# Routed attention block: the bias term of the scores summed on VectorE and brought in by two passes with ones

## The chip, the cores and the metric

The kernel runs on one core of a Trainium2 chip. The metric is the device time of one execution in microseconds (us); the median of three runs of the kernel before is 603.29 us (601.7 to 603.42).

## The reference

Four sequences of 2048 tokens of width 256 pass an attention layer and then a soft mixture of experts, each with a residual and a layer norm. All is fp32. What matters here:

```python
def _mlp(x, W1, b1, W2, b2):
    h = jax.nn.gelu(x @ W1 + b1, approximate=False)
    return h @ W2 + b2
q, k, v = (_mlp(x, ...) for each of q, k, v)
scale = np.sqrt(N_EMBD * BLOCK_SIZE).astype(np.float32)
scores = jnp.einsum('bid,bjd->bij', q, k) / scale
scores = scores * jnp.tril(jnp.ones((T, T)))          # no softmax
out = jnp.einsum('bij,bjd->bid', scores, v)
x = _layernorm(x + (layernorm of out) * ln_w + ln_b)
...
xn = _layernorm(x, ln_gamma, ln_beta)
logits = jnp.einsum('bnd,des->bnes', l2norm(xn) * scale, l2norm(mu))
dispatch = softmax(logits, over the tokens); combine = softmax(logits, over the 256 slots)
slot_in = jnp.einsum('bnd,bnes->besd', xn, dispatch)
slot_out = gelu(slot_in @ w1 + b1) @ w2 + b2
x = _layernorm(x + jnp.einsum('besd,bnes->bnd', slot_out, combine))
```

As the scores have no softmax, attention is linear: out of a token is q times the running sum of k^T v over the earlier tokens (the state), plus a part within its own chunk. The bias of q's second layer makes a term that is the same for every query: gamma_j = b2q . k_j, so each output row also gets the sum of gamma_j v_j over all earlier tokens j. That sum is what the change deals with.

## The kernel before

Tokens are cut into 64 tiles (chunks) of 128 tokens, 16 to a sequence. Four chunks make a group (512 tokens, `GT = 4`), four groups a sequence (`GB = 4`), 16 groups in all. The kernel is two blocks with a barrier of all engines between them: attention, then routing with the experts and the output. Each engine has its own program, written out by hand; order between engines comes from semaphores alone, and an engine that waits holds up all behind it.

In attention, `body(g, ...)` runs on each engine once for each group: it projects group g (hidden layers for k, q, v, then k and v themselves) and attends group a = g - 1 between these. TensorE's order is: hidden k, scores of a, hidden q, `chunk` 0, hidden v's first half, `chunk` 1, second half, k of chunks 0 and 1, `chunk` 2, k of chunks 2 and 3, `chunk` 3, v. Products are split three ways (`split3`: hi x hi, hi x lo, lo x hi, in fp32r). `chunk` adds the product with the state (`read_state`, from `state_hi` and `state_lo`, which ScalarE rounds and VectorE splits off after each `update_state`), the product of the masked scores with v (`attend_chunk`), then updates the state.

The gamma term: column D of `k_tok` is gamma. ScalarE rounds it (`gam_hi`, L607), VectorE takes the rest (`split_gamma`, L1057). `carry` (L848) runs three passes of gamma, spread over 128 columns as weights, with the 256 columns of v, into the output tile of the next chunk; ScalarE has copied the sum so far from the tile before it (`preload`, L612), so that each tile starts with the sum over all earlier chunks. VectorE then takes the statistics of the output tile pair (`pair_statistics`), weights it (`weight_out`) and adds it to x (`add_out`). GpSimd makes the low halves of the hidden v (`split_hv`), of x (`split_x`), of k (`split_ktok`) and of v (`split_v`), adds ln_b, and takes the powers for 1/sqrt (`invert_o`, and `invert_z` with `invert_x1` for the norm of z = x + attention). Twelve of the bodies stand in a hardware loop; the first two and the last two do not.

At the end of attention, `last_chunks` (TensorE) and `last_body` (VectorE) handle the last group, with the first routing steps among them: `scale_tokens(k, q)` on VectorE multiplies group k by 1/std and the routing norm's weight (L213), `add_beta` on GpSimd adds its bias (L220), `norms` on ScalarE, `floor_norms` on VectorE and `invert_norms` on GpSimd give the l2 norm, `turn_xn`, `round_xnT` and `split_xnT` turn the tokens. The last act of GpSimd in the block is `add_beta(1, 1)`, which waits for VectorE's `scale_tokens(1, 1)`. In the routing block, `route(0, first=True)` still carries what is left of groups 14 and 15: VectorE's `finish_out(15, ...)`, `shift_z` for group 14 after turning tile 3 (L1611), and ScalarE's `apply_z` of group 14 at tiles 4 to 7 (L1432), between its exponentials.

## Time and profile before

| | us |
|---|---|
| median of three runs | 603.29 |
| the profiled execution, its own time | 603.0 |
| its span | 601.3 |
| attention block | 0 to 404.3 of the span |
| routing block, experts and output | 404.3 to 601.3 |

The profiled execution is 0.3 us under the median, and 1.7 us of its time lie outside its span. The page gives the busy share of each engine and a strip of 40 slices (15 us each) with the busy tenths and TensorE's granted clock. A view by line gives the cost of one instruction; the timeline gives start, length and, in brackets, the idle time ahead of it with what ended it. Matmul lengths overlap (an entry of 0.28 us starts 0.12 us after the one ahead of it), so the cost of a pass is read from the distance of starts.

### The profile page before, as it was taken

How to read it: one execution, taken by the hardware profiler on the slowest of the kernel's cores; microseconds unless marked ns; L12 is line 12 of the kernel's file. 1: busy time of each engine (PE TensorE's matmuls, PEld its weight loads, DVE VectorE, ACT ScalarE, POOL GpSimd, SP SyncE). 2: the span in 40 equal slices, each digit the busy share in tenths (PEclk: the TensorE clock that was granted, in tenths of full speed). 3: DMA queues.
4: the chain of work that ended last, by engine and by line, in shares of the span. 5: the costliest groups of instructions: out<-in, count | busy, mean ns of one | idle time of the engine just before them, and what ended most of it. 6: DMA issues, size and time to landing. Idle time of an engine off the chain costs nothing. (4 is left out here: it accounts for less than half of the span.)

```text
span 601.3 us, 11764 instructions
## 1 busy us (share of the span) xinstructions
PE 579.7 (96%) x3844; PEld 531.7 (88%) x3844; DVE 478.5 (80%) x1012; ACT 392.8 (65%) x888; POOL 344.2 (57%) x359
## 2 busy tenths in 40 slices
PE   7989999999999999999999999977999999999995
PEld 5879999989999998999998999967899999988884
DVE  5698789788797897887978979878887777447786
ACT  3755766666767667667676766555877777535774
POOL 1738568577595585675956856466644444104443
PEclk9999999999999999999999999999899999999999
DMA  7324134042141340422413403204455555832444
GB/s 229 79 71 105 19 89 87 21 106 38 68 105 17 87 89 22 99 37 68 105 17 87 104 8 65 35 5 82 67 75 76 74 76 73 137 47 74 166 147 174
DMA packets 163473, 47.04 MB, mean 78 GB/s; under 512 B 139470, under 2 KB 159340, under 8 KB 163436
## 3 DMA queue, kind: packets, MB, share of 16 engines
q1 hardware_dynamic: 163424, 46.57, 35.4%
q8 instruction: 20, 0.33, 0.2%
q14 instruction: 17, 0.14, 0.1%
q10 hardware_dynamic: 12, 0.00, 0.0%
HBM read 21.39 MB, written 8.39 MB: 50 GB/s over the span
## 5 line engine op out<-in xcount | busy, mean ns | idle before, releaser
L511 POOL TENSOR_TENSOR h_lo<-xn_all,h_hi 128x512 fp32r<-128x512 f32 x32 | 41.4, 1292 | 114.2 <-ACT xn_all L595 114.1
L593 ACT ACTIVATE h_hi<-bank,bias_col 128x512 fp32r<-128x512 f32 x96 | 66.3, 691 | 32.9 <-PE bank L713 29.1
L711 PE MATMUL bank<-xnT_hi,w_hi 128*128 128x512 f32 x188 | 76.1, 405 | 0.0
L712 PE MATMUL bank<-xnT_lo,w_hi 128*128 128x512 f32 x188 | 74.4, 396 | 0.0
L713 PE MATMUL bank<-xnT_hi,w_lo 128*128 128x512 f32 x188 | 74.1, 394 | 0.0
L1510 PE MATMUL bank<-xn_all,e_tok 128*128 128x257 f32 x256 | 65.8, 383 | 0.0
L1084 DVE TENSOR_TENSOR state_lo<-bank,state_hi 128x512 fp32r<-128x512 f32 x57 | 39.2, 688 | 32.2 <-ACT state_hi L630 32.2
L630 ACT CAST state_hi<-bank 128x512 fp32r<-128x512 f32 x57 | 33.5, 588 | 37.1 <-PE bank L843 37.1
L1600 DVE STREAM_TRANSPOSE e_turn<-e_tok 128x256 f32<-128x256 f32 x64 | 40.5, 638 | 20.8 <-ACT e_tok L1414 20.2
L1588 PE MATMUL bank<-w_sb,ET_all 128*128 128x256 f32 x256 | 55.4, 379 | 0.0
L1414 ACT ACTIVATE e_tok<-bank,shift,xinv 128x256 f32<-128x256 f32 x64 | 36.2, 566 | 29.0 <-PE bank L1500 26.1
L1588 PEld LDWEIGHTS bank<-w_sb,ET_all 128*128 128x128 f32 x256 | 48.6, 190 | 6.6
L1498 PE MATMUL bank<-mu_hi,xnT_hi 128*128 128x256 f32 x128 | 47.5, 371 | 5.9 <-ACT e_tok L1414 3.1
L1510 PEld LDWEIGHTS bank<-xn_all,e_tok 128*128 128x128 f32 x256 | 44.5, 191 | 3.9
L237 POOL TENSOR_TENSOR xinv<-n_low,minus_half 128x4 f32<-128x4 f32 x16 | 18.2, 1140 | 51.0 <-DVE n_low L232 51.0
L517 POOL TENSOR_TENSOR ktok_lo<-xn_all,ktok_hi 128x512 fp32r<-128x512 f32 x32 | 38.2, 1194 | 11.4 <-ACT ktok_hi L610 11.4
L713 PEld LDWEIGHTS bank<-xnT_hi,w_lo 128*128 128x128 f32 x188 | 35.4, 188 | 8.7
L621 ACT CAST v_hi<-xn_all 128x512 fp32r<-128x512 f32 x32 | 19.9, 621 | 32.9 <-DVE xn_all L1064 32.9
L523 POOL TENSOR_TENSOR v_lo<-xn_all,v_hi 128x512 fp32r<-128x512 f32 x32 | 40.5, 1288 | 1.3 <-ACT v_hi L621 1.3
L506 POOL TENSOR_TENSOR x_all<-x_all,lnb_rows 128x512 f32 (+1 forms) x32 | 40.8, 1303 | 0.0
L711 PEld LDWEIGHTS bank<-xnT_hi,w_hi 128*128 128x128 f32 x188 | 35.4, 188 | 5.9
L712 PEld LDWEIGHTS bank<-xnT_lo,w_hi 128*128 128x128 f32 x188 | 35.4, 188 | 5.6
(188 smaller groups left out, 2054.3 us busy)
## 6 DMA issues: line engine op xcount, KB each, us to landing
x_all<-in_L_attn_x SPq DMA_DIRECT2D x16, 512.0 KB, 3.7
kT<-k_turn SPq DMA_DIRECT2D x128, 64.0 KB, 2.5
ET_all<-e_turn SPq DMA_DIRECT2D x64, 128.0 KB, 3.8
xn_all<-in_xT SPq DMA_DIRECT2D x15, 512.0 KB, 4.4
out<-xn_all SPq DMA_DIRECT2D x15, 512.0 KB, 3.0
w_sb<-in_L_ffn_w SPq DMA_DIRECT2D x2, 512.0 KB, 6.0
xn_all<-in_L_ffn_w SPq DMA_DIRECT2D x2, 512.0 KB, 6.8
xn_all<-in_xT SPq DMA_DIRECT2D x2, 256.0 KB, 3.8
```

The costliest lines, as they stand in the source:

```text
L506: pool.tensor_tensor(xp, xp, lnb_rows[:, :].unsqueeze(1).to_broadcast([P, 2, D]), ALU.add).then_inc(xb_ready, 1)
L511: pool.tensor_tensor(h_lo[:, V_SLOT, m, :], hv[:, m, :], h_hi[:, V_SLOT, m, :].bitcast(F32), ALU.subtract).then_inc(hv_split, 1)
L523: pool.tensor_tensor(v_lo[:, pair, :], v_tok[:, pair, :], v_hi[:, pair, :].bitcast(F32), ALU.subtract).then_inc(v_split, 1)
L593: nc.scalar.activation(h_hi[:, h_slot(j, n), m, :], ps, ACT.Gelu, bias=bias(n, m))
L711: nc.tensor.matmul(ps, w[0], xs[0], start=start, stop=False, skip_group_check=shared)
L712: nc.tensor.matmul(ps, w[0], xs[1], start=False, stop=False, skip_group_check=shared)
L713: return nc.tensor.matmul(ps, w[1], xs[0], start=False, stop=stop, skip_group_check=shared)
L1084: nc.vector.tensor_tensor(lo[:, :, :], state_halves, hi[:, :, :].bitcast(F32), ALU.subtract).then_inc(state_split, 1)
L1498: nc.tensor.matmul(ps, hi, mu_hi[:, kb, :], start=(kb == 0), stop=False)
L1510: last = nc.tensor.matmul(fold_ps(b)[s][:, 0:D + 1], e_tok[:, t % 4, s * P:(s + 1) * P], xn[q][:, t % GT, :], start=(t == 0), stop=(t == T ...
L1588: last = nc.tensor.matmul(mix_ps[k % 2][t][:, 0:D], ET_all[:, k, GT * s + t, :], so[:, k // GB, s, :], start=(s == 0), stop=(s == SB - 1))
L1600: nc.vector.transpose(e_turn[q % 2][:, :, :, t % GT, :], e_tok[:, t % 4, :].rearrange("p (s r f) -> p f s r", s=SB, f=FOUR)).then_inc(e_tu ...
```

## The change

- `carry` is now two passes. VectorE keeps `v_sum`: for each of the 128 token places the sum of gamma times v over all earlier chunks (`sum_v` and `close_sum`, one instruction of 128x256 for each chunk). ScalarE rounds it in pairs (`round_vsum`), GpSimd takes the low half (`split_vsum`), and TensorE multiplies both by a matrix of ones into the chunk's own output tile. `preload`, `gam_hi` and `split_gamma` are gone.
- `chunk` puts the carry between its other passes; for the first chunk of a sequence it updates the state first and attends second. TensorE now waits itself (`z_ready`) until the output tiles are free.
- GpSimd's body starts with `split_vsum(a, 0)`, and only then comes the power chain of z (`invert_z`, `invert_x1`), which was at the end of the body before.
- At the end of attention: tokens of group 1 are scaled on GpSimd in two instructions (`divide_tokens`, `weight_tokens`) in place of VectorE's four; `add_beta(1, 1)` moves behind the barrier, and GpSimd's `add_ln_b` for the last group one body ahead.
- In routing, VectorE's `shift_z` of group 14 comes after tile 2 (ahead of `scale_tokens(3, 3)`) and not after tile 3, and `split_xnT(1, 1)` stands ahead of `weight_out`.
- At the start, `mark_out` (two fp32 products of 512 columns) is `warm_up` (three), and the causal mask is 128 wide and not 512.

```diff
@@ gpsimd
+                def split_vsum(g, m):
+                    pool.wait_ge(vsum_rounded, 2 * g + m + 1)
+                    pair = slice(2 * m, 2 * m + 2)
+                    pool.tensor_tensor(vsum_lo[:, pair, :], v_sum[:, pair, :], vsum_hi[:, pair, :].bitcast(F32),
+                                       ALU.subtract).then_inc(vsum_split, 1)
+                def divide_tokens(k, q):
+                    pool.wait_ge(x1_ready, GT * k + 3 * GT)
+                    pool.wait_ge(r2_ready, k + 3)
+                    pool.wait_ge(hv_split, 2 * GROUPS)
+                    pool.tensor_tensor(xn[q][:, :, 0:D], x1_all[:, GT * k:GT * k + GT, :],
+                                       r2_all[:, GT * k:GT * k + GT].unsqueeze(2).to_broadcast([P, GT, D]),
+                                       ALU.mult).then_inc(tok_divided, 1)
+                def weight_tokens(q):
+                    pool.wait_ge(tok_divided, 1)
+                    pool.tensor_tensor(xn[q][:, :, 0:D], xn[q][:, :, 0:D],
+                                       g_rows[:, :].unsqueeze(1).to_broadcast([P, GT, D]), ALU.mult
+                                       ).then_inc(tok_scaled, GT)
                 def body(g, j, ba, attend=True, project=True, settle=True, more=True):
                     a = g - 1
                     if not project:
+                        split_vsum(a, 1)
+                        weight_tokens(1)
+                        return
+                    if attend:
+                        split_vsum(a, 0)
+                    if attend and settle:
+                        invert_z(pool, a - 1, j % 2)
+                        invert_x1(pool, a - 1, j % 2)
+                    split_hv(g, 0)
+                    if attend:
+                        invert_o(pool, a, 0)
+                    if not more:
+                        add_beta(pool, 0, 0)
+                    if attend:
+                        split_vsum(a, 1)
+                    split_hv(g, 1)
...
+                    if not more:
+                        divide_tokens(1, 1)
+                    split_ktok(g, 0)
...
-                    if attend and project and more:
-                        invert_z(pool, a, (j - 1) % 2)
-                        invert_x1(pool, a, (j - 1) % 2)
@@ scalar
-                    nc.scalar.copy(gam_hi[:, :], k_tok[:, :, D]).then_inc(gam_rounded, 1)
-                def preload(ba, i):
...
+                def round_vsum(g, m):
+                    act.wait_ge(v_summed, GT * g + 2 * m + 1)
+                    pair = slice(2 * m, 2 * m + 2)
+                    nc.scalar.copy(vsum_hi[:, pair, :], v_sum[:, pair, :]).then_inc(vsum_rounded, 1)
                     hidden(g, j, WK1, 0)
+                    if attend:
+                        round_vsum(a, 0)
                     hidden(g, j, WK1, 1)
...
                         follow(0)
+                    if attend:
+                        round_vsum(a, 1)
@@ tensor
-                def carry(a, ba, i):
...
+                def carry(a, c, start):
+                    pe.wait_ge(vsum_split, 2 * a + c // 2 + 1)
+                    if isinstance(a, int) and a == 0 and c == 1:
+                        pe.wait_ge(ones_rounded, 1)
+                    nc.tensor.matmul(out_tile(c), ones_r[:, :], vsum_hi[:, c, :], start=start, stop=False,
+                                     skip_group_check=True)
+                    nc.tensor.matmul(out_tile(c), ones_r[:, :], vsum_lo[:, c, :], start=False, stop=False,
+                                     skip_group_check=True)
                 def chunk(a, ja, ba, c, p):
                     i = GT * ja + c
-                    if 0 < i < TB - 1:
-                        pe.wait_ge(preloaded, PB * ba + i)
                     if i == 0:
-                        pe.wait_ge(z_ready, GT * a + 2)
+                        update_state(a, c, True)
+                    if c % 2 == 0:
+                        pe.wait_ge(z_ready, GT * a + c + 2)
+                    if i == 0:
                         last = attend_chunk(a, c, True, True)
                     elif c == 0:
-                        read_state(ba, i, c, p, False)
+                        read_state(ba, i, c, p, True, False)
+                        carry(a, c, False)
                         last = attend_chunk(a, c, False, True)
                     else:
-                        attend_chunk(a, c, False, False)
-                        last = read_state(ba, i, c, p, True)
+                        attend_chunk(a, c, True, False)
+                        carry(a, c, False)
+                        last = read_state(ba, i, c, p, False, True)
@@ vector
-                def split_gamma(g):
...
+                def sum_v(g, j, c):
+                    dve.wait_ge(v_biased, 2 * g + c // 2 + 1)
+                    if not (isinstance(g, int) and g == 0):
+                        dve.wait_ge(v_summed, GT * g + c)
+                        dve.wait_ge(vsum_split, 2 * g)
...
+                        last = nc.vector.scalar_tensor_tensor(out=v_sum[:, c + 1, :], in0=v_tok[:, c, :], scalar=gamma,
+                                                              in1=v_sum[:, c, :], op0=ALU.mult, op1=ALU.add)
...
+                    if attend:
+                        sum_v(a, ja, 1)
+                        sum_v(a, ja, 2)
                     split_h(g, j, WQ1, 0)
...
                         follow(0)
+                        close_sum(a, ja)
                     split_h(g, j, WQ1, 1)
...
-                    split_gamma(g)
+                    sum_v(g, j, 0)
@@ routing
+                add_beta(pool, 1, 1)
                 invert_o(pool, GROUPS - 1, 0)
...
-                        if first and t == 3:
+                        if first and t == 2:
                             shift_z(dve, a - 1, 1 - p)
```

## Rows read from the trace of the kernel before

**Rows 1.** The page's second part: TensorE's busy tenths in 40 slices of the span

```profile
PE   7989999999999999999999999977999999999995
```

**Rows 2.** Stretches: busy us (count) of PE, PEld, DVE, ACT, POOL; clock; DMA

```profile
280.00:300.00 20.00, 20.00 (x146) 18.77 (x146) 17.64 (x39) 13.47 (x27) 15.66 (x17) 1.00 0.33 79
```

**Rows 3.** Timeline of TensorE: one carry of three passes, and what follows it

```profile
206.37 0.28 PE L711 MATMUL bank<-v_hi,gam_hi 128*128 128x256 f32 x1
...
206.71 0.40 PE L711 MATMUL bank<-xnT_hi,w_hi 128*128 128x512 f32 x1
```

**Rows 4.** Groups by line, 0 to 400 us: busy, mean ns of one | idle before

```profile
L713 PE MATMUL bank<-v_hi,gam_lo 128*128 128x256 f32 x60 | 16.6, 277 | 0.0
...
L213 DVE SCALAR_TENSOR_TENSOR xn_all<-x_all,r_all,g_rows 128x256 f32<-128x256 f32 x4 | 1.7, 476 | 0.0
```

**Rows 5.** VectorE's gam_lo: duration ns min/median/max

```profile
L1057 DVE TENSOR_TENSOR gam_lo<-xn_all,gam_hi x16: 340/354/1297, 26.6 to 391.1; 128x4 fp32r<-128x4 f32 x16
```

**Rows 6.** Timeline of VectorE, from gam_lo to the state of the next chunk

```profile
222.48 1.28 DVE L1057 TENSOR_TENSOR gam_lo<-xn_all,gam_hi 128x4 fp32r<-128x4 f32 x1
...
227.35 0.69 DVE L1079 TENSOR_TENSOR masked_lo<-bank,masked_hi 128x512 fp32r<-128x512 f32 x1
...
230.26 0.69 DVE L1084 TENSOR_TENSOR state_lo<-bank,state_hi 128x512 fp32r<-128x512 f32 x1 [1.06 <-ACT state_hi L630]
```

**Rows 7.** Timeline of GpSimd, the same stretch

```profile
222.45 2.51 POOL L523 TENSOR_TENSOR v_lo<-xn_all,v_hi 128x512 fp32r<-128x512 f32 x2
...
227.16 1.01 POOL L205 TENSOR_TENSOR r_all<-ve_x,minus_half 128x4 f32 x1 [0.18 <-POOL ve_x L203]
232.73 1.28 POOL L511 TENSOR_TENSOR h_lo<-xn_all,h_hi 128x512 fp32r<-128x512 f32 x1 [4.57 <-ACT xn_all L595]
...
236.26 1.30 POOL L511 TENSOR_TENSOR h_lo<-xn_all,h_hi 128x512 fp32r<-128x512 f32 x1 [1.45 <-ACT xn_all L595]
```

**Rows 8.** Timeline of TensorE: chunk 1 reads the state

```profile
231.54 0.28 PE L711 MATMUL bank<-state_hi,h_hi 128*128 128x256 f32 x1
```

**Rows 9.** Timeline of TensorE: first chunk of a sequence, with the wait ahead of it

```profile
132.22 0.38 PE L711 MATMUL bank<-v_hi,masked_hi 128*128 128x256 f32 x1 [0.19 <-DVE masked_lo L1079]
```

**Rows 10.** Timeline of GpSimd at the end of attention and over the barrier

```profile
401.86 2.17 POOL L220 TENSOR_TENSOR xn_all<-xn_all,b_rows 128x1024 f32<-128x1024 f32 x1 [3.51 <-DVE xn_all L213]
404.34 0.20 POOL L1355 MEMSET blank<- 128x1 f32 x4 [0.31 <-POOLq L261]
```

**Rows 11.** Timeline of TensorE: last pass of attention, first of routing, two waits in it

```profile
401.78 0.28 PE L713 MATMUL bank<-v_hi,masked_lo 128*128 128x256 f32 x1
404.58 0.36 PE L1498 MATMUL bank<-mu_hi,xnT_hi 128*128 128x256 f32 x1 [2.53 <-POOL blank L1355]
...
420.51 0.39 PE L1498 MATMUL bank<-mu_hi,xnT_hi 128*128 128x256 f32 x1 [3.06 <-ACT e_tok L1414]
...
422.97 0.58 PE L1498 MATMUL bank<-mu_hi,xnT_hi 128*128 128x256 f32 x1 [0.35 <-DVE xnT_lo L257]
```

**Rows 12.** Stretches of 4 us at the start of routing, columns as in rows 2

```profile
404.00:408.00 4.00, 3.42 (x17) 3.45 (x18) 3.55 (x9) 2.00 (x8) 1.49 (x11) 0.61 0.64 142
...
420.00:424.00 4.00, 3.14 (x15) 2.42 (x16) 3.91 (x9) 4.00 (x13) 0.41 (x1) 0.74 0.76 110
424.00:428.00 4.00, 4.00 (x24) 3.68 (x24) 2.94 (x8) 3.35 (x12) 2.62 (x6) 0.83 0.15 19
```

**Rows 13.** Timelines of VectorE, GpSimd and ScalarE where z of group 14 is shifted

```profile
417.47 1.80 DVE L181 SCALAR_TENSOR_TENSOR nm_z<-st_z,r_z 128x4 f32<-128x4 f32 x1
...
417.09 2.17 POOL L220 TENSOR_TENSOR xn_all<-xn_all,b_rows 128x1024 f32<-128x1024 f32 x1
...
419.31 0.60 ACT L189 ACTIVATE x_all<-x_all,nm_z,r_z 128x256 f32<-128x256 f32 x1 [5.27 <-DVE nm_z L181]
```

**Rows 14.** Timeline of TensorE at the start

```profile
2.98 3.78 PE L776 MATMUL bank<-causal,ident 128*128 128x512 f32 x4 [2.98 <-POOL causal L491]
...
7.25 1.96 PE L724 MATMUL bank<-xnT_hi,w_hi 128*128 128x512 f32 x4 [0.28 <-ACT bias_col L647]
```

166 lines of the change are left out of this document (82 added, 84 removed).

## The prediction, made before the changed kernel was run

> **What bounds the kernel now.** I read the busy strip first: TensorE is at nine tenths or more in nearly every slice from the third to the twenty-fifth, dips to seven once, around 400 us, and is full again after [rows 1]. The stretches say how full: in attention TensorE is busy 20.00 of 20 us at the whole clock, while VectorE has some 17.6, ScalarE 13.5, GpSimd 15.7 [rows 2]. So inside attention a pass that TensorE no longer runs is time won, as long as no other engine comes too late; and what the others get or lose matters only through their lateness. Then I read the timeline for the exceptions. In the first chunk of a later sequence TensorE waits 0.19 us for the masked scores [rows 9]. At the barrier between the blocks it stands from 402.06 (401.78 + 0.28) to 404.58; soon after, for 3.06 us ahead of 420.51, and for 0.35 us ahead of 422.97 [rows 11]. The clock, whole (2.4 GHz) in attention, is granted at 0.61 over the 4 us after the first long wait and at 0.74 and 0.83 over those after the second: part of each is spent at the lower level of 1.2 GHz [rows 12].
>
> **The change part by part.**
>
> *The passes.* A carry of three passes starts at 206.37 and the next work at 206.71: 0.34 us [rows 3], or 0.115 us a pass. 60 carries run before, as each of the three passes stands 60 times [rows 4]. After, again 60 (15 of 16 chunks, four sequences), of two passes: two passes of the same 256 columns. The starts of neighbours are 0.115 to 0.12 us apart, so 0.235 us. 60 x (0.343 - 0.235) = **-6.5 us** (ends: -6.3 and -6.9).
>
> *VectorE.* gone: `gam_lo`, 16 times, 0.34 us at least and 1.30 at most [rows 5]. New: one instruction for each chunk, nearest row `scale_tokens`, 128x256 of two SBUF tensors, 0.476 us, 0.41 from start to start in a row of four [rows 4]. Of four in a group one stands in gam_lo's place; three fill idle time: ahead of the split of hidden q, and after the state's split, where VectorE idles 1.06 us [rows 6].
> What of it is late? gam_lo needs 0.08 us of work but took 1.28: it started at 222.48, 0.03 us after GpSimd's v_lo (two of 1.26 us from 222.45), and ended as the first of these ended [rows 6, 7]. An instruction of VectorE that reads two tensors of SBUF stands until GpSimd's running one is over. The new sums are of that kind. The one in gam_lo's place inherits that wait and adds 0.4 us of work, so the masked scores, at the end of the same unbroken run of VectorE, come 0.4 us later: 228.44 and not 228.04 [rows 6]. TensorE wants them after reading the state, near 228.7: it fits by 0.25 us. Two more sums follow (0.85 us), the split of hidden q (0.6), then the state: without waits VectorE is there at 229.9, ScalarE hands over the rounded state at about 230.7 (230.26 + 0.4), so the state is split at 231.35. TensorE reads it at 231.54 [rows 8], 0.11 us earlier after the change (0.345 of passes go ahead of it, 0.235 come): 231.43. GpSimd's power chain runs 1.7 us later than now (the new split of 1.29 ahead of it and 0.4), so its last power of 1.01 us [rows 7] can fall on the second sum and cost up to 1 us, of which about 0.8 is free. I take 0.04 us in each of 14 groups, **+0.5** (ends 0 and +4).
>
> *First chunks.* The state update now goes ahead of the masked product, so the 0.19 us [rows 9] go, three times, -0.5. But there is no reading of the state ahead of chunk 0 there, so the state of chunk 1 is wanted 0.6 us sooner than in other groups, and the same 0.4 us make it late by 0.2 to 0.5: +0.6. Together **+0.1**. In the very first attended group VectorE also has the routing matrix to split; the two sums delay the state by about 0.25 us: **+0.25**.
>
> *ScalarE and GpSimd.* ScalarE loses 56 copies and 16 small ones and gets 32 of about 0.6 us in idle time; the first of each group stands ahead of the second half of hidden k, which is wanted only after the masking. GpSimd gets 32 splits of 1.29 us (like v_lo), 2.6 us a group: one ahead of the power chain, where 4.57 us of idle time follow, one ahead of the second `split_hv`, where it idles 1.45 [rows 7]. Behind the first wait (for ScalarE) stand only z's powers, wanted on VectorE 4 us later. I take nothing; without that cover they would cost 2.6 us a group.
>
> *The start.* `warm_up` is three fp32 products for two: 3.78 us for two [rows 14], so 1.9 more, begun 0.6 us sooner as the mask is smaller. First hidden starts at about 8.3 and not 7.25 [rows 14], but its four passes then may run at the whole clock (1.96 us now, half that). **+0.3** (ends -0.3 and +1).
>
> *The last group.* GpSimd's list is fuller: `divide_tokens` (2.2 us, like `add_beta`, [rows 10]), ln_b and the splits of the sums. `round_vsum` of group 15 stands on ScalarE ahead of the first turned tokens and the state, and waits for its sum: the state of the second chunk comes 1.1 us later. TensorE, whose chain there already runs from state to state, ends that much later, less the passes saved and what it waits for now: **+0.8** (ends 0 and +2).
>
> *The barrier.* Now GpSimd's add_beta (401.86 to 404.03) is last, and routing starts 0.31 us later, TensorE 0.24 after that [rows 10, 11]. After, add_beta is behind the barrier, the token scaling ends near 402.3, and TensorE itself is last. Its gap of 2.52 us becomes 0.31 + 0.24, some 0.6: **-1.9** (ends -2.2 and -1).
>
> *Opening of routing.* VectorE is the bound from 410 to 423. `shift_z` took 1.80 us for four columns, because GpSimd's add_beta ran from 417.09 to 419.26, and ScalarE stood 5.27 us for it [rows 13]. One tile earlier it meets only short steps of the powers: -1.5 on VectorE. ScalarE is free 3.6 us sooner, but then TensorE waits for VectorE's split of group 2's tokens, so 3.06 + 0.35 of waiting shrink by 1.5 and not by 3.4. Against that, add_beta(1) now starts with VectorE's `scale_tokens(2, 2)` and can hold it 2.2 us, of which 0.7 lands in VectorE's run (the rest in its idle places); TensorE waits 1.3 us for the turned tokens where now it runs slowly: **-0.8** (ends -3.1 and +1.5).
>
> The Trainium skill (SBUF, State Buffer, section on SBUF's two separate sides) says that GpSimd and a VectorE operation with two SBUF inputs share a port pair as an exclusive lock, held for a whole instruction, whoever starts first. That speaks against putting sums on VectorE and splits on GpSimd. By that rule the trace agrees (gam_lo, and `shift_z`), and the sum above already has it; its full reach is rival C.
> The skill (TensorE: Matmul & The Clock Gate, Part 1) has the clock fall to half with idleness; by that rule the trace agrees at both long waits [rows 11, 12]; shorter waits would make it rival A, and 592.1.
>
> *Sum.* -6.5 + 0.5 + 0.1 + 0.25 + 0.3 + 0.8 - 1.9 - 0.8 = -7.25. On the profiled execution's 603.0 that gives 595.75; the median of the runs is 0.3 higher: **596.0**.
>
> **The rivals.**
> A. *The clock stays whole and the opening runs through.* The lowered clock costs 4 x 0.39 = 1.6 us after the first long wait and 4 x (0.26 + 0.17) = 1.7 after the second [rows 12]. If the shorter waits leave the clock up, and VectorE isn't held by add_beta, the opening gives 3.1 and one stretch of lowered clock 1.6 more: 596.0 - 2.3 - 1.6 = 592.1. Against it: 2.5 us of waiting remain ahead of group 2.
> B. *Half of the gain is waited away.* The state's split is late by 0.3 us in each of 14 groups (+4.2): 600.2, with the tail at its upper end 601.5. For it: the margin in an ordinary group is 0.1 us. Against: 0.8 us of VectorE's idle time is there for a wait.
> C. *Slower.* Both sums after the masks wait out a GpSimd instruction each (1.29 for the new split, or a power of 1.01) and the masked scores come after their 0.25 us of margin. Two whole waits are 2.3 us, 0.8 free: 1.5 us late, 14 times 21 us less the repair by later slack, at 0.9 a group 12.6: about 608. The decision point is 0.45 us of lateness a group, where the 6.5 us are gone. Against: the power chain's short steps leave gaps, and v_lo is over by then.
> D. *It doesn't do what it says.* TensorE's time doesn't follow the passes (the ones product costs more than a pass with v, or other waits close up behind it): 603.
>
> **How the numbers follow.** Forecast (594 to 598) 0.50; A (591.5 to 594) 0.13; B (598 to 601.5) 0.22; D 0.08; C 0.07. The range 593.0 to 600.5 holds the forecast, the nearer parts of A and most of B, about 0.8. A measurement of this kernel tells 0.3% (1.8 us) from no change: faster (under 601.5) 0.85, same 0.08, slower 0.07.
>
> **What would show it.** Passes: in the steady stretches TensorE stays at 20.00 of 20 us and a group takes 0.43 us less. Masks and state: a wait of TensorE for state_lo in the list of waits, over 1 us in total, is B; over 10 us, C. Barrier: gap under 1 us. Opening: nm_z of group 14 under 0.4 us, ScalarE's wait for it gone, TensorE's longest wait there on the split of the tokens. Start: first hidden near 8.3 us. The prediction is wrong if VectorE's sums take far more than 0.5 us each, or if the ones product's starts are more than 0.12 us apart.

## The result

| | before | changed |
|---|---|---|
| median of the runs | 603.07 (5 runs) | 598.42 (5 runs) |
| lowest to highest | 601.70 to 603.42 | 596.35 to 598.54 |
| profiled execution, its own time | 603.0 | 598.5 |
| its span | 601.3 | 596.8 |

The changed kernel takes 0.9914 of the time before, 95% interval 0.9891 to 0.9938: 4.65 us less, where 7.1 were forecast. The page's strip of busy tenths of TensorE and of its granted clock, 40 slices of 15 us (before: [rows 1]):

```profile
PE   8989999999999999999999999887999999999995
...
PEclk9999999999999999999999999999899999999998
```

The same bound as before: TensorE is full through attention and dips at the border to the routing. The stretches of the changed kernel (columns: busy us and count of PE, PEld, DVE, ACT, POOL, then clock, DMA share and GB/s); the first answers to [rows 2], the last stands at the same clock times as one of [rows 12]:

```profile
280.00:300.00 20.00, 20.00 (x143) 18.73 (x142) 18.34 (x39) 13.75 (x25) 18.27 (x19) 1.00 0.35 79
...
416.00:420.00 4.00, 1.85 (x7) 1.78 (x8) 4.00 (x10) 2.02 (x8) 1.56 (x2) 0.74 0.81 112
420.00:424.00 4.00, 4.00 (x24) 3.60 (x23) 2.47 (x7) 2.98 (x10) 2.68 (x6) 0.83 0.48 66
```

TensorE still has 20.00 of 20 us, GpSimd has gone from 15.66 to 18.27, VectorE from 17.64 to 18.34. The new work by groups of lines, from 0 to 400 us (busy us, mean ns of one, idle time before it):

```profile
L882 PE MATMUL bank<-vsum_hi,ones_r 128*128 128x256 f32 x60 | 17.0, 283 | 2.1 <-POOL vsum_lo L531 2.1
L884 PE MATMUL bank<-vsum_lo,ones_r 128*128 128x256 f32 x60 | 16.9, 281 | 0.0
...
L531 POOL TENSOR_TENSOR vsum_lo<-v_sum,vsum_hi 128x512 fp32r<-128x512 f32 x32 | 41.3, 1289 | 0.6 <-ACT vsum_hi L641 0.6
...
L1107 DVE SCALAR_TENSOR_TENSOR v_sum<-xn_all,v_sum 128x256 f32<-128x256 f32 x44 | 24.3, 552 | 2.7 <-DVE v_sum L1107 1.3
```

60 carries of two passes, and GpSimd's split keeps TensorE waiting for 2.1 us in all.

**Where the 4.5 us of span come from.** I cut both spans at TensorE's starts of the scores of each group, at the first pass of the routing, and at the first pass behind the routing's last long wait. The forecast for each stretch is the prediction's own sum, its passes laid out by stretch: a carry before is 0.343 us, after 0.235, so a group whose chunks carry four times on both sides gains 0.43. In a sequence's first group four carries become three (0.67), in its last group three become four (0.09).

| stretch | before | changed | difference | forecast |
|---|---|---|---|---|
| start to the first scores | 29.04 | 29.40 | +0.36 | +0.3 |
| first attended group | 26.21 | 26.48 | +0.27 | -0.4 |
| 13 groups of the steady part | 312.55 | 308.37 | -4.18 | -4.7 |
| group with the last projections | 22.39 | 24.09 | +1.70 | -0.4 |
| last scores to TensorE's end in attention | 11.87 | 12.26 | +0.39 | +0.7 |
| that end to the first pass of the routing | 2.52 | 0.53 | -1.99 | -1.9 |
| to the pass behind the last long wait | 18.39 | 17.02 | -1.37 | -0.8 |
| the rest | 178.33 | 178.65 | +0.32 | 0 |

So one stretch misses by 2.1 us, the groups of the steady part by 0.5, the first attended group by 0.7, and the opening of the routing does better by 0.6.

One of these differences is hardly the change's. Behind the barrier the profile before has some 3 us at the half clock (1.2 GHz) [rows 12]. A run further down, the kernel before without the third pass of its carries, has the same routing code and waits 2.63 us at the barrier, and there the clock stays whole. Its first pass of the routing, its pass behind the last long wait, and its stretch behind the barrier (columns as in rows 2):

```profile
398.22 0.36 PE L1500 MATMUL bank<-mu_hi,xnT_hi 128*128 128x256 f32 x1 [2.63 <-POOL blank L1357]
...
415.34 0.58 PE L1500 MATMUL bank<-mu_hi,xnT_hi 128*128 128x256 f32 x1 [0.39 <-DVE xnT_lo L257]
...
398.00:402.00 4.00, 3.78 (x31) 3.73 (x31) 3.91 (x10) 2.79 (x10) 1.80 (x10) 1.00 0.78 167
```

That is 17.12 us where the table has 18.39 for the kernel before (the run with full weights has 17.12 too). So 1.27 of the opening's 1.37 us are the lower clock of the execution before. With the clock whole behind the barrier on both sides the opening gained 0.1.

The experiments take the stretches in turn. Each experiment is set against the changed kernel's profile or against the kernel before on the same chip.

### The profile page after: what moved, and what is told of

Read it like the earlier page. It is cut to its first block and busy times, and to the rows that moved or that the text cites. A ratio compares the mean times of both kernels' runs of the same rounds, so it can differ in the third digit from the quotient of the medians.

```text
span 596.8 us, 11673 instructions
## 1 busy us (share of the span) xinstructions
PE 575.5 (96%) x3786; PEld 527.4 (88%) x3786; DVE 490.3 (82%) x1054; ACT 390.9 (65%) x848; POOL 391.8 (66%) x393
## 5 line engine op out<-in xcount | busy, mean ns | idle before, releaser
L1471 ACT ACTIVATE e_tok<-bank,shift,xinv 128x256 f32<-128x256 f32 x64 | 36.1, 564 | 31.3 <-PE bank L1557 25.7
L525 POOL TENSOR_TENSOR v_lo<-xn_all,v_hi 128x512 fp32r<-128x512 f32 x32 | 42.7, 1354 | 1.3 <-ACT v_hi L646 1.3
L531 POOL TENSOR_TENSOR vsum_lo<-v_sum,vsum_hi 128x512 fp32r<-128x512 f32 x32 | 41.3, 1289 | 0.6 <-ACT vsum_hi L641 0.6
```

The lines of the kernel that those rows point to most:

```text
L525: pool.tensor_tensor(v_lo[:, pair, :], v_tok[:, pair, :], v_hi[:, pair, :].bitcast(F32), ALU.subtract).then_inc(v_split, 1)
L531: pool.tensor_tensor(vsum_lo[:, pair, :], v_sum[:, pair, :], vsum_hi[:, pair, :].bitcast(F32), ALU.subtract).then_inc(vsum_split, 1)
```

## The experiments

### The group with the last projections

GpSimd (POOL) and TensorE (PE) of the changed kernel, timelines:

```profile
375.87 2.20 POOL L220 TENSOR_TENSOR xn_all<-xn_all,b_rows 128x1024 f32<-128x1024 f32 x1
378.02 1.28 POOL L531 TENSOR_TENSOR vsum_lo<-v_sum,vsum_hi 128x512 fp32r<-128x512 f32 x1
...
379.35 0.39 PE L882 MATMUL bank<-vsum_hi,ones_r 128*128 128x256 f32 x1 [1.68 <-POOL vsum_lo L531]
```

In this group alone `add_beta` of group 0 (2.20 us) stands ahead of the split that TensorE's third chunk reads. In a steady group that split ends only 0.36 us ahead of the pass that reads it (changed kernel):

```profile
210.46 1.29 POOL L531 TENSOR_TENSOR vsum_lo<-v_sum,vsum_hi 128x512 fp32r<-128x512 f32 x1
...
212.11 0.28 PE L882 MATMUL bank<-vsum_hi,ones_r 128*128 128x256 f32 x1
```

The experiment only swaps the two:

```diff
-                    if not more:
-                        add_beta(pool, 0, 0)
                     if attend:
                         split_vsum(a, 1)
                     split_hv(g, 1)
+                    if not more:
+                        add_beta(pool, 0, 0)
```

> The changed kernel with one reorder: in the body of the last group GpSimd adds beta of group 0 (2.20 us) behind the split of the sums and the hidden v, not ahead of them. Theory (a wait of 1.68 us at chunk 2 of that body is lost for good, as the body took 24.09 us where 22.39 stood before): that body takes 22.4 us or less and the time falls by 1.5 to 1.9 us against the changed kernel. Rival (later work, the turned tokens of group 0 above all, wants beta so soon that the wait moves there): the time falls by under 0.5 us.

Measured: 595.95 us (4 runs; before, on the same chip, 602.41), 0.9889 of the kernel before, 0.9846 to 0.9932; span 594.0. The same timelines:

```profile
375.14 1.29 POOL L531 TENSOR_TENSOR vsum_lo<-v_sum,vsum_hi 128x512 fp32r<-128x512 f32 x1
...
377.75 2.21 POOL L220 TENSOR_TENSOR xn_all<-xn_all,b_rows 128x1024 f32<-128x1024 f32 x1
...
376.79 0.28 PE L882 MATMUL bank<-vsum_hi,ones_r 128*128 128x256 f32 x1
```

The wait is gone and the group takes 22.16 us instead of 24.09. Nothing behind it gives that back. The +1.70 is this order of two instructions.

### What the pass itself is worth

The kernel before, with the third pass of each carry (`gam_lo` times `v_hi`) left out; its carried term lacks that small part:

```diff
-                    split3(out_tile((i + 1) % GT),
-                           (gam_hi[:, c:c + 1].to_broadcast([P, P]), gam_lo[:, c:c + 1].to_broadcast([P, P])),
-                           (v_hi[:, c, :], v_lo[:, c, :]), False, False, shared=True).then_inc(carried, 1)
+                    gam = gam_hi[:, c:c + 1].to_broadcast([P, P])
+                    nc.tensor.matmul(out_tile((i + 1) % GT), gam, v_hi[:, c, :], start=False, stop=False,
+                                     skip_group_check=True)
+                    nc.tensor.matmul(out_tile((i + 1) % GT), gam, v_lo[:, c, :], start=False, stop=False,
+                                     skip_group_check=True).then_inc(carried, 1)
```

> The kernel before with the third pass of each carry (low half of gamma times v) left out, so a small part of the carried sum is missing; nothing is added to VectorE, ScalarE or GpSimd. This is what the pass alone is worth. Theory: 60 x 0.115 = 6.9 us less, all of it, because TensorE never waits in attention: 596.2. Rival (other engines close up behind TensorE): less than 4 us.

Measured: 596.92 us (8 runs, 595.05 to 599.69; before, on the same chip, 602.41), 0.9906 of the kernel before, 0.9881 to 0.9932; the profiled execution is one of the fast ones, 595.35, with a span of 593.6 against 601.3. The groups of 24.33 us take 23.87: there a pass that goes is won in full, 0.115 us each. In the first group of a later sequence the wait for the masked scores takes 0.1 of 0.46 us back. From the first to the last scores 57 passes bring 6.09 us, 0.107 each, and 60 at that are 6.4, close to the forecast's 6.5; the medians differ by 5.5. The gain of the changed kernel's steady group, 24.33 to 24.11, is half of that. Something else in the group must have become slower, and without a wait: in the list of what TensorE waited for in the changed kernel, from 29 to 376 us (us in total, times, longest), all three are in the first attended group:

```profile
PE bank L873 <- DVE x_all L1159: 1.4, 1, 1.4
PE bank L742 <- DVE state_lo L1135: 0.5, 1, 0.5
PE bank L844 <- DMA kT<-k_turn: 0.2, 1, 0.2
```

### The pace of the passes around the carry

The cause shows in the distance of starts. v's projection is 24 passes of 256 columns; its first pass and the pass behind its last, before:

```profile
241.86 0.28 PE L711 MATMUL bank<-w_hi,h_hi 128*128 128x256 f32 x1
...
244.58 0.40 PE L711 MATMUL bank<-xnT_hi,w_hi 128*128 128x512 f32 x1
```

and in the changed kernel:

```profile
239.72 0.28 PE L742 MATMUL bank<-w_hi,h_hi 128*128 128x256 f32 x1
...
242.58 0.39 PE L742 MATMUL bank<-xnT_hi,w_hi 128*128 128x512 f32 x1
```

2.72 us and 2.86, 113.3 ns and 119.2 ns a pass, the same passes at the same clock. In the kernel before, ten of the 13 steady groups have the fast pace, and the groups on either side of them. The three without a carry ahead of the projection have 117.9 there. k's projection (12 passes of 258 columns, twice a group) went from 120.0 to 122.5 ns. Added up from start to start over one group of 24.33 us, the carries fell from 1.37 to 0.95 us, v's projection rose from 2.72 to 2.86, k's two from 2.87 to 2.94, and all other passes together changed by less than 0.01: -0.43 and +0.21 are the -0.22. Five runs look for the reason: weights of one column spread over 128 ahead of the projection, or the addresses of the buffers, which moved with the new ones and the smaller mask.

The kernel before, with full weights in the carry (a block of k's tokens in gamma's place, so the carried term is another quantity):

```diff
-   (gam_hi[:, c:c + 1].to_broadcast([P, P]), gam_lo[:, c:c + 1].to_broadcast([P, P])),
+   (ktok_hi[:, c, 0:P], ktok_lo[:, c, 0:P]),
```

> The kernel before, with the carry's three passes on a full 128x128 block of k as weights and not on gamma spread from one column; the carried term is thus something else than the reference asks. Theory (spread weights ahead of v's projection make its fast pace): the carry takes 0.36 us and not 0.345, the projection of v 2.86 us and not 2.72, and a group 24.50 us and not 24.33. Rival (what makes the pace is a carry standing there, its pass into the output bank, whatever its weights): 2.72 and 24.33 stay.

Measured: 604.38 us (one run), span 602.7. v's projection has 117.9 ns everywhere, the group 24.50 us instead of 24.33. So in the kernel before, the carry's weights right ahead of it do make the fast pace.

The changed kernel, with a spread column of ones:

```diff
-                    nc.tensor.matmul(out_tile(c), ones_r[:, :], vsum_hi[:, c, :], start=start, stop=False,
+                    nc.tensor.matmul(out_tile(c), ones_r[:, 0:1].to_broadcast([P, P]), vsum_hi[:, c, :], start=start, stop=False,
```

(and the same for `vsum_lo`).

> The changed kernel, the matrix of ones read as one column spread over 128 (stride 0), as gamma was before. In the kernel before, the 24 passes of v's projection start 0.1133 us apart where a carry of spread gamma stands right ahead of them, and 0.1185 where none does; in the changed kernel 0.119 always. Theory 1 (the spread weights themselves run faster): the carry's two passes take 0.230 us and not 0.24, the projection stays at 0.119 because reading and updating the state stand between. Theory 2 (spread weights anywhere in the chunk put TensorE in a faster pace for what follows): the projection of v falls to 0.1133 and a group to 23.96 us. Rival (pace has nothing to do with weights): nothing changes, group 24.11.

Measured: 597.93 us (one run), span 596.2; the projections stay at 119.2 and 122.5 ns, a group is 24.05 instead of 24.11, by slightly closer starts of the state's reading and update (0.02 us each) and of the carries (0.01). Only in the three groups that end a sequence, with no update of the state ahead of v's projection, does that go to 118.7. Here the carry doesn't stand right ahead of v's projection, the state's reading does. So the next run puts every fourth chunk's carry there (`carry_last` is the carry's two passes with a spread column of ones):

```diff
+                    elif c == GT - 1:
+                        attend_chunk(a, c, True, False)
+                        read_state(ba, i, c, p, False, False)
+                        if i < TB - 1:
+                            update_state(a, c, False)
+                        carry_last(c).then_inc(chunk_done, 1)
+                        return
```

> The changed kernel, with the carry of every fourth chunk put back where the kernel before had its own: behind the state's update, right ahead of v's projection, and with one column of ones spread over 128 as its weights. Theory 1 (the 113 ns passes of v's projection come from spread weights right ahead of them): the projection is back at 113 ns a pass and 2.72 us in the groups that have this carry, against 2.86 us in the changed kernel; a group of kind 1 and 2 goes from 24.11 to 23.97 us, three of four groups gain 0.14 us, and the span falls by some 1.5 us (10 to 11 groups). Theory 2 (addresses of the buffers, which the change moved, set the pace of v's projection): it stays at 119 ns, and the groups stay at 24.11.

Measured: 597.65 us (one run), span 595.9. The projection goes to 118.5 ns and not to 113.3. The first theory falls in this form.

The addresses: the new buffers behind the others, and small ones of the same total size in their place, so that all buffers of hidden layers and chunks stand where they stood before the change (not all of the moved declarations are shown).

```diff
-            v_sum = asb("v_sum", [P, GT, D])
-            vsum_hi = asb("vsum_hi", [P, GT, D], F32R)
-            vsum_lo = asb("vsum_lo", [P, GT, D], F32R)
-            ones_r = asb("ones_r", [P, P], F32R)
+            warm = asb("warm", [P, GT])
+            mu_n2 = asb("mu_n2", [P, SB])
+            mu_inv = asb("mu_inv", [P, SB])
...
             causal = asb("causal", [P, P])
+            ones = asb("ones", [P, P])
+            mu_diag = asb("mu_diag", [P, SB, P])
...
             state_lo = asb("state_lo", [P, KB, D], F32R)
-            warm = asb("warm", [P, GT])
+            v_sum = asb("v_sum", [P, GT, D])
+            vsum_hi = asb("vsum_hi", [P, GT, D], F32R)
+            vsum_lo = asb("vsum_lo", [P, GT, D], F32R)
+            ones_r = asb("ones_r", [P, P], F32R)
...
```

> The changed kernel with its new buffers (the sums, their halves, the ones) declared behind the others and small ones put in their place, so that the hidden layers' buffers stand at the addresses of the kernel before. Theory 2 (addresses set the pace): k's projection, 122.5 ns a pass in the changed kernel and 120.0 before, goes back to 120.0 (-0.03 us on each of two stretches a group, -0.06 a group, -0.8 in all), and v's from 119.2 to 117.9 (-0.03 a group). Theory 1 (only the order of the passes and their weights matter): both stay at 122.5 and 119.2, and the group stays at 24.11.

Measured: 595.38 us (one run), span 593.7. First pass of a k projection and the pass behind its last, changed kernel and then this run:

```profile
210.28 0.28 PE L742 MATMUL bank<-m_hi,h_hi 128*128 128x258 f32 x1
...
211.75 0.29 PE L742 MATMUL bank<-v_hi,masked_hi 128*128 128x256 f32 x1
```

```profile
208.94 0.28 PE L742 MATMUL bank<-m_hi,h_hi 128*128 128x258 f32 x1
...
210.38 0.28 PE L742 MATMUL bank<-v_hi,masked_hi 128*128 128x256 f32 x1
```

k's projection is back at 120.0 ns, v's at 117.9, the group at 24.05 and 23.33 (24.11 and 23.39). From first to last scores that is 0.74 us (386.58 - 28.38 = 358.20, against 358.94). That part of the loss was the addresses. The rest of the 3.1 us of span is a shorter start (28.38 against 29.40, which differs from run to run: 28.2 to 29.5 in the kernels with this start) and the clock, below.

Both together, with the edits of the run on `add_beta` and of one on the routing (below):

> The changed kernel with four edits at once: the add of beta of group 0 behind the two splits; the split of transposed group 2 ahead of the statistics in the routing; the hidden layers' buffers at the addresses of the kernel before; and every fourth chunk's carry last, with a spread column of ones, right ahead of v's projection. The runs so far show that a spread carry right ahead gave 113 ns passes in the kernel before and only 118.7 in the changed one. If that was because the addresses were others (the two causes act together), the projection is now at 113.3 ns and 2.72 us in 11 groups, a group of kind 1 and 2 takes 23.92 us, and the median is some 1.2 us under that of the next run, near 592.3. If the fast passes have to do with the gamma weights or with v as what is moved through, and not with the spread alone, they stay at 117.9, the group at 24.04, and the median is that of the next run.

Measured: 593.49 us (4 runs; before 601.88), 0.9855 of the kernel before, 0.9836 to 0.9874. Last pass of the carry, first of v's projection, and the pass behind its last:

```profile
262.44 0.28 PE L882 MATMUL bank<-vsum_lo,ones_r 128*128 128x256 f32 x1
262.56 0.29 PE L742 MATMUL bank<-w_hi,h_hi 128*128 128x256 f32 x1
...
265.37 0.39 PE L742 MATMUL bank<-xnT_hi,w_hi 128*128 128x512 f32 x1
```

2.81 us: 117.1 ns, against 117.9 without a spread carry ahead at these addresses. The spread alone and the old addresses don't bring 113.3 back. What is left is what the kernel before had and no run of the changed one has: gamma's own column as the weights, v as what is moved through, or the next chunk's output tile as the target. Which of the three is open, as no run separates them, and why TensorE's starts should hang on any is open too. The size is known: 24 x 4.6 ns, 0.11 us, in ten groups of the steady part, 1.1 us.

### Is GpSimd's order in the steady group needed?

The change puts the split of the first sums ahead of z's powers. Put back:

```diff
-                    if attend:
-                        split_vsum(a, 0)
                     if attend and settle:
                         invert_z(pool, a - 1, j % 2)
                         invert_x1(pool, a - 1, j % 2)
+                    if attend:
+                        split_vsum(a, 0)
```

> The changed kernel with GpSimd's z chain (3.1 to 3.3 us in all) ahead of the split of the first sums, as the kernel before had it at a group's end. Rival C of the prediction, that TensorE gets its operands too late once GpSimd has more ahead of them: the split then starts when the chain has ended, some 3.3 us later than now; its lead over the pass that reads it (split's end 201.66, pass at 204.14: 2.5 us) turns into a wait of 0.6 to 1.0 us in each group whose first chunk carries (11 groups), none in the others, where the second chunk reads it 5.9 us after the scores' start: the span is 6 to 10 us longer, 604 to 607, which takes back all that the change gave. If the margin is larger than that (nothing is late), the span stays at 596.8.

Measured: 609.69 us (one run), span 608.0, 11.2 more than the changed kernel and 6.7 more than the kernel before. GpSimd and TensorE, and TensorE's line in the list of waits from 29 to 390 us:

```profile
207.07 1.01 POOL L205 TENSOR_TENSOR r_all<-ve_x,minus_half 128x4 f32 x1 [0.18 <-POOL ve_x L203]
208.04 1.43 POOL L531 TENSOR_TENSOR vsum_lo<-v_sum,vsum_hi 128x512 fp32r<-128x512 f32 x1
...
209.52 0.39 PE L882 MATMUL bank<-vsum_hi,ones_r 128*128 128x256 f32 x1 [0.77 <-POOL vsum_lo L531]
```

```profile
PE bank L882 <- POOL vsum_lo L531: 8.5, 11, 0.8
```

11 waits of 0.77 us, and each such group is 1.0 longer (24.11 to 25.13), so a wait costs a third more than the list says: around it the starts are further apart (the state's six passes with the wait take 1.64 us instead of 0.71, the carry 0.35 instead of 0.24). The groups without such a wait lose 0.2. With this order the change is slower than no change, which is rival C of the prediction at another place: the sums' split, not the masks, behind GpSimd's powers.

### The barrier and the opening of the routing

TensorE at the end of attention and in the opening, changed kernel, only the rows with a wait (before: [rows 11]):

```profile
392.98 0.39 PE L873 MATMUL bank<-v_hi,ktok_hi 128*128 128x256 f32 x1 [1.22 <-DVE h_lo L1135]
394.43 0.36 PE L882 MATMUL bank<-vsum_hi,ones_r 128*128 128x256 f32 x1 [0.47 <-POOL vsum_lo L531]
401.13 0.36 PE L1555 MATMUL bank<-mu_hi,xnT_hi 128*128 128x256 f32 x1 [0.53 <-POOL blank L1411]
...
403.52 0.55 PE L245 MATMUL bank<-ident,xn_all 128*128 128x128 f32 x3 [0.73 <-POOL xn_all L220]
...
418.15 0.58 PE L1555 MATMUL bank<-mu_hi,xnT_hi 128*128 128x256 f32 x1 [2.55 <-DVE xnT_lo L257]
```

*The add of beta put back ahead of the barrier:*

```diff
                         weight_tokens(1)
+                        add_beta(pool, 1, 1)
                         return
...
-                add_beta(pool, 1, 1)
                 invert_o(pool, GROUPS - 1, 0)
```

> The changed kernel with the add of beta of group 1 put back ahead of the barrier between attention and routing, on GpSimd, behind the product with gamma. Theory (prediction: the barrier's gap of 2.52 us was this add, and moving it takes 1.9 of it away): the add takes 2.2 us before the barrier, the first logits pass comes 1.9 to 2.2 us later, TensorE's gap at the barrier goes from 0.53 to some 2.5; behind it the 0.73 us wait for the transposed group's beta goes, and VectorE's scale of four tiles falls from 3.62 us to 1.7, so that the net loss is 1 to 1.5 us. Rival: the gap has another floor (the barrier itself, or the product with gamma), and the first pass moves by less than 0.5 us.

Measured: 597.21 us (one run), span 595.5. Its GpSimd, TensorE and VectorE:

```profile
399.37 2.19 POOL L220 TENSOR_TENSOR xn_all<-xn_all,b_rows 128x1024 f32<-128x1024 f32 x1
...
402.12 0.36 PE L1555 MATMUL bank<-mu_hi,xnT_hi 128*128 128x256 f32 x1 [1.67 <-POOL blank L1412]
...
401.91 1.67 DVE L213 SCALAR_TENSOR_TENSOR xn_all<-x_all,r_all,g_rows 128x256 f32<-128x256 f32 x4 [2.52 <-PEq L261]
```

From the last scores to the routing's first pass it takes 13.94 us against 12.79: the move is worth 1.15 at the barrier, not the 1.9 that the prediction gave it. The gap is 1.67 here and was 2.53 before [rows 11], though the add is the same and stands at the same place. Before, it ended 1.97 us after TensorE's last pass (404.03 against 402.06, [rows 10, 11]), here 1.11 us (401.56 against 400.45): the tokens' scaling ahead of it is two GpSimd products, the first made long before, and no longer VectorE's. That is the other 0.8 of the 1.99. Behind the barrier the changed kernel pays the add: 0.73 us of TensorE's wait, and VectorE's scaling of four tiles, which takes 1.67 us here, runs from 400.93 to 404.55 there. To the pass behind the last long wait it is 16.17 us against 17.02. Net, the move brought 0.3 us. That this run's span is 1.3 us under the changed kernel's is the clock again: no half clock falls in behind its wait of 2.55 us, where the changed kernel's profile has it (below).

*The shift of group 14 one tile later, as before:*

```diff
-                        if first and t == 2:
+                        if first and t == 3:
                             shift_z(dve, a - 1, 1 - p)
```

> The changed kernel with group 14's shift (nm_z) put back to the fourth token tile of the routing, where it was before. If the earlier place made the gain of the opening (prediction, with 0.8 us in all and 0.4 of it for the shift): the shift starts behind the scale of four tiles and meets GpSimd's add of beta, so it takes 1.8 us instead of 0.12; ScalarE waits some 3 to 5 us for it instead of 1.5, and the stretch from the first logits pass to the pass behind the last big wait, 17.02 us in the changed kernel and 18.39 before, is 18.2 to 18.5: the span is 1.2 to 1.5 us over that of the changed kernel. Rival: the gain of the opening comes from the split of the second transposed group going ahead of pair 0's output and from the beta that went before the barrier; then the stretch stays within 0.4 us of 17.02.

Measured: 599.33 us (one run), span 597.6. VectorE and ScalarE, of the changed kernel and then of this run:

```profile
412.40 0.12 DVE L181 SCALAR_TENSOR_TENSOR nm_z<-st_z,r_z 128x4 f32<-128x4 f32 x1
...
412.56 0.60 ACT L189 ACTIVATE x_all<-x_all,nm_z,r_z 128x256 f32<-128x256 f32 x1 [1.50 <-DVE nm_z L181]
```

```profile
413.31 1.80 DVE L181 SCALAR_TENSOR_TENSOR nm_z<-st_z,r_z 128x4 f32<-128x4 f32 x1
...
412.93 2.17 POOL L220 TENSOR_TENSOR xn_all<-xn_all,b_rows 128x1024 f32<-128x1024 f32 x1
...
415.15 0.60 ACT L189 ACTIVATE x_all<-x_all,nm_z,r_z 128x256 f32<-128x256 f32 x1 [5.27 <-DVE nm_z L181]
```

The same four columns, 0.12 and 1.80 us, and the long one ends with GpSimd's add (412.93 + 2.17 = 415.10). The eleventh token tile of the routing starts 24.42 us after the first instead of 22.48. The half clock lasts longer in this run, some 7 us against 3:

```profile
416.00:420.00 4.00, 3.65 (x13) 0.50 0.72 104
```

(416 to 420 us: busy us and count of PE, clock, DMA share, GB/s.) But the delay is VectorE's and not the clock's: its split for the ninth tile ends 18.81 us after the first pass, and 16.96 in the changed kernel. So the shift's place is worth 1.9 us. The moved add of beta takes 0.85 of it back. If the two simply add up, the rest of the change costs another 0.9 in the opening, as at the same clock only 0.1 is left; no run takes that apart. The Trainium skill (SBUF, State Buffer, section on SBUF's two separate sides) has GpSimd and a VectorE instruction with two SBUF inputs share a port pair as an exclusive lock for a whole instruction. By that rule the trace agrees in each of these pairs (1.80 us against 0.12 for the shift, 3.62 against 1.67 for the scaling), and it is what to look for when four columns take as long as an instruction of another engine.

*The split of group 2's tokens ahead of the statistics.* The 2.55 us ahead of 418.15 are VectorE's: it runs two statistics and a transpose first. The experiment has the edit on `add_beta` of group 0 too:

```diff
                         if first and t == 4:
+                            split_xnT(dve, 2, 2)
+                        if first and t == 4:
                             z_summed(dve, a, 0)
...
-                        if t % GT == 1 and not (last and q == GB - 1) and not (first and q == 0):
+                        if t % GT == 1 and not (last and q == GB - 1) and not (first and q <= 1):
                             split_xnT(dve, k + 1, (q + 1) % GB)
```

> The changed kernel with two edits that the traces point to. One is that of the run before on this matter (the add of beta of group 0 behind the two splits that TensorE waits for). The other: in the routing of group 0, VectorE splits the transposed tokens of group 2 right behind the fifth transpose, ahead of the two z statistics and the sixth transpose, which stand ahead of it now (0.67 + 0.63 + 0.67 us, for which TensorE waits 2.55 us at 418.15). Expected: against the changed kernel -1.7 us from the first (as measured), and -1.5 to -3 from the second: the wait falls to about 0.6 us, and the clock, half in the passes behind it now, stays whole; the span 591.5 to 593, the median near 593.5, 0.984 of the kernel before. Rival: the statistics of group 15 come 1.2 us later, and with them its scale and r; a wait of the third or fourth group takes the place of the one removed, and the span stays at 594.

Measured: 594.80 us (4 runs; before, on the same chip, 603.05), 0.9855, 0.9833 to 0.9877. TensorE waits less:

```profile
415.16 0.38 PE L1555 MATMUL bank<-mu_hi,xnT_hi 128*128 128x256 f32 x1 [0.82 <-DVE xnT_lo L257]
```

But the rival held for most of it. The ninth tile starts 15.28 us after the first instead of 17.00 (the run with the old addresses, which like this one has no half clock in this part), the seventeenth 31.10 instead of 31.27. Of 1.7 us won at one wait, 0.2 are left eight tiles on: VectorE has the same work ahead of the next group's norms, whose `n_low` starts 17.45 us after the first pass here (417.33) and 17.42 in the changed kernel (418.55), and GpSimd's power and ScalarE's exps wait for that. With the shorter wait the clock stays whole there in all three profiles with this edit; it does so too in three without it, below.

The same with the old addresses and without the carry moved:

> The same without the fourth edit: the add of beta later, the split first, the old addresses. Expected from the runs of these edits alone: 594.8 for the first two, and 0.06 us a group less, 0.8 in all, for the addresses: a median of 594.0, 0.985 of the kernel before, and 592 where no stretch at the half clock falls in (one costs some 1.5 to 2 us), 595.5 where one does.

Measured: 593.74 us (4 runs), 0.9857, 0.9838 to 0.9876, within 0.3 us of the forecast for it. The pair of these runs (593.49 with the carry last, 593.74 without) can't be told apart in time.

### The clock

TensorE's granted clock in the opening, run with `add_beta` of group 0 moved, then the split first with old addresses (columns: busy us and count of PE, clock, DMA share, GB/s):

```profile
412.00:416.00 4.00, 1.44 (x7) 0.89 0.56 78
416.00:420.00 4.00, 4.00 (x23) 0.68 0.46 64
```

```profile
412.00:416.00 4.00, 3.17 (x21) 1.00 0.58 80
416.00:420.00 4.00, 3.91 (x27) 1.00 0.45 63
```

Behind the wait of 2.55 us the passes start 0.21 us apart (the level of 1.2 GHz) for some 3 us, then 0.12 again. Such a stretch costs 1.5 us: the seventeenth tile comes 32.8 us after the first with it (changed kernel and the run on `add_beta`), 31.3 without (old addresses). It isn't there in every execution: that last run has the same 2.55 us wait, and the clock stays whole, as it does in the runs with the spread column of ones and with beta put back. At the barrier it is the same: the three profiles with the old routing wait 2.50, 2.53 and 2.63 us there, and the clock falls behind the 2.53 alone. And in the profiled run with the split first one such stretch is at another place, behind the waits of the last group (392 to 396 at 0.57). The changed kernel's five runs fall in two sets by it: 598.4 to 598.5 at a mean granted clock of 0.993, three times, and 596.35 and 596.55 at 0.996, twice. It isn't all that differs between executions: of the eight runs without the third pass both 595.35 and 599.69 are at 0.993. The Trainium skill (TensorE: Matmul & The Clock Gate, Part 1) has the clock fall with idleness; the runs here agree that it falls only behind waits, and show that equal waits do not always bring it down.

## Why the prediction was right, and where not

- **The forecast, 596.0, range 593.0 to 600.5.** 598.42 is in the range, at the border of the forecast's own band (594 to 598) and rival B's. B's cause, a state split that is late in 14 groups, did not come. The 2.4 us that were missing have other causes. Of the 4.5 us of span that the two profiles differ by, 1.27 are the clock behind the barrier, so the code's part there is nearer to 3.2.
- **The passes, -6.5.** Right in size: 60 carries of two passes, 0.118 us a pass, and the run without the third pass shows 0.107 to 0.115 us a pass arriving. The step that failed is the one beside it: I took the neighbours' pace as given. The projections behind became slower, v's by 4.6 ns a pass with gamma's carry gone and 1.3 ns by the new addresses, k's by 2.5 ns by the addresses. That is 1.1 + 0.7 us in the steady part, more than all of the 0.5 by which it misses.
- **VectorE, +0.5.** Too high. Its working starts from a `gam_lo` that was held for 1.28 us, while 11 of the 16 take 0.34 to 0.39 [rows 5]; the 0.08 us that it gives as gam_lo's own work stands in no row. The sums take 0.48 us each where nothing holds them (0.55 on average with the held ones), as their row said, the masks were never late, and the state only once, by 0.47 us, in the first attended group. Without the two pace effects the 13 groups would have come out 1.3 us better than forecast.
- **First chunks, +0.1.** Too high: a sequence's first group fell from 24.05 to 23.15 us, by 0.90, where 0.67 are passes. The wait went and no other came. It was worth more than the 0.19 us that the row gives: in these groups before, the hidden layers and the first masked product took 0.45 us longer than in the others, and the slower projections took 0.21 back.
- **First attended group, +0.25.** About a quarter of what came (0.94): with the 0.67 of its passes the stretch should have fallen by 0.4, and it rose by 0.27. TensorE waits 1.44 us for the routing's matrix as it did before (1.47), and then 0.47 for the state, with 0.1 more in the passes behind that wait; its projections take 0.22 us more.
- **ScalarE and GpSimd, nothing.** Right in 14 groups, wrong in one, and that was the largest single miss: 2.1 us. The step read GpSimd's idle time from a steady group and took it for all. In the group with the last projections `add_beta(0, 0)` now stands ahead of the second split and holds TensorE for 1.68 us. Its 2.2 us were in the rows and its new place in the diff. The steady part held by less than that: its second split has 0.36 us of lead. The first one has 2.5 us (it ends at 201.66, the pass that reads it starts at 204.14), and the run with z's powers first shows that 3.3 us less of it costs 11.2 us.
- **Start, +0.3.** The first hidden layer starts at 8.25, as said, and its four passes take 1.23 us, not 1.96, as said. The end of this stretch varies by 1.3 us among kernels with the same start, so +0.36 tells little.
- **Last group, +0.8.** +0.39 with the passes in it; within its ends.
- **Barrier, -1.9.** -1.99, right in sum, and for partly the wrong reason: the moved add gives 1.15, and 0.85 of that comes back behind the barrier.
- **Opening, -0.8.** -1.37, and that it came out on this side is luck: 1.27 are the clock of the execution before, and at the same clock 0.1 us was gained. The shift at 0.12 us and ScalarE's wait of 1.50 are as said, and its worth, 1.9 us, is above the 1.5. The step that failed is what stood against it: the 0.7 us for the moved add are 0.85, and 0.9 more go to something that the sum doesn't have and no run names.
- **Rival A, the clock.** It comes true in two of five runs of the changed kernel by its clock part alone; I had it as one state of the kernel, and it is a matter of single executions. The stretch behind the barrier is in none of the eleven profiles of the changed kernel and its variants, whose waits there are 0.53 or 1.67 us; as two of the three with the old routing lack it too, whether the change removes it is open.

The version with all that was found, 593.49 us, is 0.9855 of the kernel before, where the changed kernel is 0.9914: about half of the difference of some 3.6 us is one swap of GpSimd instructions (1.9 us).

## What to carry to other kernels

Where an engine is full, a pass taken out of it is won nearly in full, and what remains is to look at the order of the queues that feed it, in each special body (first, last, drain) as well as in the loop: the same split was in time by 0.36 us in the steady groups, and TensorE waited 1.7 us for it in the one where a 2.2 us instruction had been put ahead. Read the lead of each operand, not the idle time of its engine. A wait at one place is worth what is left of it some tiles on, not its length: 1.7 us at the ninth tile were 0.2 at the seventeenth. And before a difference under 2 us is explained by code, look at the granted clock of both executions: 1.27 of the opening's 1.37 us were that.

## What the runs showed of the hardware that I had not expected

- The same 24 fp32r passes of 256 columns at the whole clock start 113.3, 117.1, 117.9, 118.5, 118.7 or 119.2 ns apart, the same from group to group, by what stands ahead of them and by the addresses of their buffers; 12 passes of 258 columns 120.0 or 122.5, by the addresses alone.
- A stretch of some 3 us at 1.2 GHz behind a wait of 2.55 us comes in some executions and not in others, and costs 1.5 us.
- A wait of 0.77 us costs a full group 1.0 us, and one of 0.19 us cost 0.45.
